# Router logits of five iterations computed with the experts stationary, four token tiles side by side on the output partitions

## What is computed

```
scores = jax.nn.softmax(xf @ Wg, axis=-1)          # Wg is 128 x 32: one column an expert
weights, indices = jax.lax.top_k(scores, TOP_K)     # TOP_K = 4 of 32 experts
...                                                 # each expert takes its first 512 token pairs
out = swiglu(xg, W1[e], W2[e], W3[e]) * w[:, None]
y = y.at[tok].add(out)
z = swiglu(xf, Ws1, Ws2, Ws3)                       # a shared expert
return (y + z)
```

## Time and profile before

| | |
|---|---|
| median of 3 runs | 824.46 us (823.9 to 824.59) |
| the profiled execution | 823.99 us, of which the span of instructions is 822.3 us |
| TensorE products (PE) | 805.6 us busy, 98% of the span |
| VectorE (DVE) | 655.5 us, 80% |
| GpSimd (POOL) | 600.2 us, 73% |
| ScalarE (ACT) | 548.9 us, 67% |
| TensorE clock granted | 1.000 of full speed over the span |

### The profile page before, as it was taken

How to read it: one execution, slowest core, us unless ns; L and a number is a source line. 1 busy time by engine, 2 the same in 40 slices (tenths; PEclk the granted TensorE clock), 3 DMA queues, 4 the chain that set the end, 5 groups by cost and what they waited for, 6 DMA issues and landing times.

```text
span 822.3 us, 12552 instructions
## 1 busy us (share of the span) xinstructions
PE 805.6 (98%) x3782; PEld 603.3 (73%) x3782; DVE 655.5 (80%) x1533; ACT 548.9 (67%) x1016; POOL 600.2 (73%) x469
## 2 busy tenths in 40 slices
PE   7899999999999999999999999999999999999997
PEld 4577877667677676777778777777777768888775
DVE  5886777898897988988787877969778899775664
ACT  3577677767567767679474985749665775777453
POOL 2168778767857677588776886877887787968775
PEclk9999999999999999999999999999999999999999
DMA  9152625425254063450544507254252534415552
GB/s 321 25 129 70 139 52 106 103 59 112 52 106 111 18 142 68 97 120 18 121 101 106 129 10 159 54 132 116 61 128 72 123 74 106 111 51 113 124 115 73
DMA packets 49331, 80.73 MB, mean 98 GB/s; under 512 B 3280, under 2 KB 14544, under 8 KB 48880
## 3 DMA queue, kind: packets, MB, share of 16 engines
q1 hardware_dynamic: 48976, 79.72, 41.8%
q10 hardware_dynamic: 288, 0.20, 0.1%
HBM read 75.19 MB, written 4.72 MB: 97 GB/s over the span
## 4 chain that ended last, share of the span: by engine, by line
PE 82%; DVE 9%; POOL 4%; issue 3%; ACT 1%; DMA 0%; POOLq 0%; DVEq 0%; ACTq 0%
PE py L869 9%; PE pb L845 7%; PE pa L845 7%; PE pb L846 7%; PE pa L846 7%; PE pb L847 7%; PE pa L847 7%; PE py L874 5%; PE py L875 4%; PE py L876 4%; PE pu L1098 3%; POOL m_h L490 3%; PE pu L970 1%; PE pv L946 1%; PE pq L1056 1%
## 5 line engine op out<-in xcount | busy, mean ns | idle before, releaser
L490 POOL TENSOR_TENSOR m_h<-m_v,m_wb 128x512 f32<-128x512 f32 x256 | 347.0, 1366 | 126.8 <-DVE m_v L1221 50.2
L580 ACT ACTIVATE m_th<-pa 128x512 f32<-128x512 f32 x240 | 141.9, 595 | 141.3 <-PE pa L847 133.7
L1221 DVE TENSOR_TENSOR m_v<-m_th,pb 128x512 f32<-128x512 f32 x224 | 151.2, 677 | 35.8 <-ACT m_th L580 16.6
L845 PE MATMUL pa<-m_xh,w1h 128*128 128x512 f32 x272 | 149.3, 549 | 0.3 <-issue 0.3
L337 POOL TENSOR_TENSOR m_hl<-m_h,m_hh 128x512 fp32r<-128x512 f32 x84 | 109.8, 1307 | 38.0 <-ACT m_hh L745 37.8
L745 ACT ACTIVATE m_hh<-m_h 128x512 fp32r<-128x512 f32 x171 | 106.9, 626 | 23.3 <-POOL m_h L490 20.4
L845 PE MATMUL pb<-m_xh,w3h 128*128 128x512 f32 x272 | 114.0, 419 | 0.9 <-DVE m_v L1221 0.7
L846 PE MATMUL pa<-m_xl,w1h 128*128 128x512 f32 x272 | 107.8, 396 | 0.0
L846 PE MATMUL pb<-m_xl,w3h 128*128 128x512 f32 x272 | 107.7, 396 | 0.0
L847 PE MATMUL pa<-m_xh,w1l 128*128 128x512 f32 x272 | 107.5, 395 | 0.0
L847 PE MATMUL pb<-m_xh,w3l 128*128 128x512 f32 x272 | 107.5, 395 | 0.0
(11 more groups left out here) (273 smaller groups left out, 1618.4 us busy)
## 6 DMA issues: line engine op xcount, KB each, us to landing
m_wb<-w_scratch SPq DMA_DIRECT2D x126, 512.0 KB, 6.7
x_sb<-in_x SPq DMA_DIRECT2D x8, 256.0 KB, 6.7
m_wb<-in_w SPq DMA_DIRECT2D x2, 1024.0 KB, 7.6
x_out<-x_sb SPq DMA_DIRECT2D x7, 256.0 KB, 6.7
u_scratch<-t_u SPq DMA_DIRECT2D x6, 256.0 KB, 2.5
t_u<-u_scratch SPq DMA_DIRECT2D x6, 256.0 KB, 2.8
f_kk<-in_w SPq DMA_DIRECT2D x1, 1024.0 KB, 10.5
w_scratch<-r_wT SPq DMA_DIRECT2D x16, 64.0 KB, 1.5
```

What stands on the lines that cost most here:

```text
L490: pool.tensor_tensor(hidden(g, p), gated(g, p), m_wb[:, p % (GRING * GP), :], ALU.mult).then_inc(sig["m_h"], 1)
L580: ins = act.activation(m_th[:, p % 2, :], pa[p % 2][:, :], ACT.Silu)
L845: pe.matmul(ps[:, :], high[:, p, :], xh, start=True, stop=False)
L1221: dve.tensor_tensor(gated(g, p), m_th[:, r, :], pb[r][:, :], ALU.mult).then_inc(sig["m_v"], 1)
```

## The change

In the five iterations with modes 4, 5 and 6 the logits products swap their operands. Before, a tile of 128 tokens was the stationary operand and the 32 columns of wg were streamed; the result lay with tokens on the partitions. Now wg is stationary (128 x 32), a tile of 128 tokens is streamed, and the four tiles go to output partitions 0 to 31, 32 to 63, 64 to 95 and 96 to 127. ScalarE copies the 128x128 result to a piece of r_wT (called r_lT in the code), and TensorE turns it back with one transpose into the next 128 columns of the same bank, where VectorE reads it. The slots of the steps behind it move.

```diff
+BY_COLUMNS = tuple(g + 1 for g in range(2 * B - 1) if MODES[g] in (4, 5, 6))
...
+        r_lT = r_wT[:, P:2 * P]
...
-                if slot == (31, 30, 32, 30, 25, 38, 23, 21)[mode]:
+                if slot == (32, 26, 29, 30, 25, 33, 21, 28)[mode]:
+                    if q in BY_COLUMNS:
+                        act.wait_ge(sig["r_lgps"], q + 1)
+                        act.activation(r_lT, router_bank(cmix)[:, 0:P], ACT.Copy).then_inc(sig["r_lT"], 1)
+                if slot == (31, 30, 32, 30, 27, 38, 23, 21)[mode]:
                     act.wait_ge(sig["r_lg"], q + 1)
...
-                        ins = pe.matmul(ps[:, E * t:E * (t + 1)], r_xT[:, P * t:P * (t + 1)], wg[:, :],
-                                        start=True, stop=True)
+                        tokens = r_xT[:, P * t:P * (t + 1)]
+                        if q in BY_COLUMNS:
+                            ins = pe.matmul(ps[E * t:E * (t + 1), 0:P], wg[:, :], tokens, start=True, stop=True)
+                        else:
+                            ins = pe.matmul(ps[:, E * t:E * (t + 1)], tokens, wg[:, :], start=True, stop=True)
                     ins.then_inc(sig["r_lgps"], 1)
+                if slot == (34, 28, 31, 32, 27, 35, 23, 28)[mode]:
+                    if q in BY_COLUMNS:
+                        pe.wait_ge(sig["r_lT"], BY_COLUMNS.index(q) + 1)
+                        pe.transpose(ps[:, P:2 * P], r_lT, ident[:, :]).then_inc(sig["r_lgt"], 1)
...
-                if slot == (30, 24, 29, 28, 22, 32, 17, 26)[mode]:
-
-                    dve.wait_ge(sig["r_lgps"], q + 1)
-                    lg = router_bank(cmix)[:, 0:T * E].rearrange("p (t e) -> p t e", t=T)
+                if slot == (30, 24, 29, 28, 27, 35, 23, 26)[mode]:
+
+                    if q in BY_COLUMNS:
+                        dve.wait_ge(sig["r_lgt"], BY_COLUMNS.index(q) + 1)
+                    else:
+                        dve.wait_ge(sig["r_lgps"], q + 1)
+                    at = P if q in BY_COLUMNS else 0
+                    lg = router_bank(cmix)[:, at:at + T * E].rearrange("p (t e) -> p t e", t=T)
...
-                if slot == (32, 29, 32, 35, 25, 38, 22, 28)[mode]:
+                if slot == (32, 29, 32, 35, 27, 38, 23, 28)[mode]:
                     dve.wait_ge(sig["r_ex"], q + 1)
...
-                if slot == (38, 34, 36, 39, 32, 38, 22, 28)[mode]:
+                if slot == (38, 34, 36, 39, 32, 38, 23, 28)[mode]:
                     constants_set()
```

More of the change, by code:

```diff
@@ L232, in hybrid_kernel @@
             "a_stats a_mvs a_vedone a_rstd a_sh a_xn a_tr a_xT a_gps a_vps a_g a_v a_s a_mx a_nm a_exp a_pT a_pTs a_o a_ri a_add "
-            "r_stats r_mvs r_vedone r_rstd r_nm r_xn r_tr r_xT m_xh m_xl r_lgps r_mx r_lg r_ex r_sum r_ri r_p r_top r_pad r_rep "
+            "r_stats r_mvs r_vedone r_rstd r_nm r_xn r_tr r_xT m_xh m_xl r_lgps r_lT r_lgt r_mx r_lg r_ex r_sum r_ri r_p r_top r_pad r_rep "
             "r_sel r_ws r_cnt r_pos r_w r_carry r_wTps r_wT w_out "
```

## The result

| | before | changed |
|---|---|---|
| median of 5 runs of each | 824.46 us (823.9 to 826.21) | 829.77 us (827.95 to 830.81) |
| the profiled execution | 823.99 us, span 822.3 | 827.95 us, span 826.1 |
| TensorE, VectorE, ScalarE, GpSimd busy | 98, 80, 67, 73% | 97, 79, 66, 72% |

The changed kernel is 0.47% slower: the ratio is 1.0047, 95% interval 1.0029 to 1.0065. The sign is as forecast; the size is not. The median is 2.7 us above the forecast of 827.1 and 0.8 above the top of its range. Execution against execution, the loss is 4.0 us where 2.7 were forecast.

The account below looks back on a forecast made before the run. TensorE's stream was taken to bound the kernel. Losses of 2.5 us (iterations 7, 9, 11), minus 0.15 (13), plus 0.38 (14) gave +2.7: 826.7 profiled, 827.1 us median (0.47 above the profiled execution before rounding), range 823.3 to 829.0.

Parts of the forecast that it names:

- d: What the new logits form takes off TensorE's four products, which ran 0.80 us as eight passes; taken as +0.26 us.
- the overlap in steps: Logits passes: a tile's second pass waits for its first, the next tile begins with that second pass; 5 x 0.107 = 0.54 us.
- The turn, 0.11: Transposing the logits back on TensorE costs 0.11 us per iteration: 0.34 to the second product after, against a 0.23 step.
- The copy costs nothing: ScalarE's copy of the logits fits in idle time or ahead of a later wait; without that cover 0.31 us.
- Iterations 7, 9 and 11, steps 1 to 7: Chain from unit 9's gate product through late exponential, a_xn, f_h and f_xl to the key product; loses 0.84 us an iteration.
- Iteration 13, the step that failed: In iteration 13 the exponential stays, its table load is already waited for, the chain to f_xl keeps order; gain 0.15 us.
- Iteration 14: VectorE has no room, so m_v(8) comes late and unit 10's linear product waits for it; loss 0.38 us.
- no overlap with a drain as well: First rival (groups don't overlap) with array drains added; put near +4.9 us when setting the range's top.
- Full overlap with the chain late: Rival: all four groups overlap fully (d = 0.59), the chain late all the same; +1.1 us, 825.6 us, chance 0.13.
- No overlap: Rival: logits groups don't overlap, or the array drains on both sides (d = -0.06); +4.4 us, 828.8 us, chance 0.15.
- The chain doesn't bind: Rival: passes overlap in steps and no wait opens; five gains of 0.15, -0.8 us, 823.7 us, chance 0.16.
- Faster: Rival: the chain doesn't bind and groups overlap fully; 5 x 0.48 = -2.4 us, 822.1 us, chance 0.10.

Follow-up runs that it names:

- experiment 5: As experiment 4, with logits, copy and turn of iterations 7, 9, 11 and 14 one place earlier and the maximum where it stood before the change: 826.17 us, ratio 1.0014.
- Experiment 8: Kernel before the change, with only ScalarE's exponential of iterations 7, 9 and 11 moved behind m_th(9): 828.22 us, ratio 1.0036.
- experiment 2: Changed kernel with the exponential of iterations 7, 9 and 11 back ahead of m_th(9), and VectorE's maximum and sum two places earlier: 830.27 us, ratio 1.0058.
- experiment 4: Changed kernel with the turn one place earlier, exponential and sum at their old places, and the maximum earlier: 825.94 us, ratio 1.0010.
- experiment 6: Changed kernel with the old logits form and old place of the maximum in iteration 13 alone: 827.49 us, ratio 1.0029.
- experiment 11: Kernel before the change, unchanged, profiled again: 824.39 us, with a TensorE wait of 1.05 us for m_v in iteration 11.
- experiment 7: Changed kernel with VectorE's sum of iterations 7, 9 and 11 moved behind m_v(9) and a_nm: 828.57 us in one run.
- the first profile: Kernel before the change, unchanged, as first profiled: execution 823.99 us.
- experiment 3: Changed kernel with all four token tiles sent to the same 32 output partitions: 830.16 us in one run.
- experiment 9: As experiment 5, with VectorE instead of ScalarE making the copy of the logits: 826.41 us, ratio 1.0019.

## Why the forecast was right in sign and short in size

- **What bounds the kernel.** Right. Nearly all of the loss is waits that opened in TensorE's stream.
- **d, and the overlap in steps.** Mis-sized: 0.26 was taken, 0.33 measured, from two errors of opposite sign. The passes took 0.35 us, not 0.54, so groups overlap more than my order of pairs allows, though less than the 0.21 of full overlap; and the entry into the narrow form costs 0.10, for which the sum had no term. That the two errors nearly cancel in d is luck. The Trainium skill (TensorEngine Tiling (Array Packing), Key Properties) says that changing the tiling mode drains TensorE. What there could be of it here is 0.10 us on entry and 0.02 on exit, less than the 0.16 each that I gave it. No run separates the entry gap from other reasons for it.
- **The turn, 0.11.** 0.12 measured.
- **"The copy costs nothing."** True in the changed kernel, where m_th(9) behind it waits 1.29 us for TensorE anyway. False in experiment 5, where the copy stands ahead of the table load.
- **Iterations 7, 9 and 11, steps 1 to 7.** Right. Gate product of unit 9 to key product: 13.25 forecast, 13.32 measured, 12.15 before. The loss was forecast at 0.84 each and measured at 0.89 in 9 and 11, 1.03 in 7. Experiment 8 shows the edit that makes it. What the steps missed is the second limit, VectorE's list, where operations are lengthened beside GpSimd. In the changed kernel it is r_sel:

```profile
423.93 1.00 DVE L1385 TENSOR_SCALAR r_sel<-r_rep 128x128 bf16<-128x128 f32 x1
```

  It cost nothing on top, but in experiment 2, where r_sel and r_ws are both lengthened, it is why the obvious repair does nothing.
- **Iteration 13, the step that failed:** "the exponential stays where it was and its table load is already waited for; the chain to f_xl keeps its order. Gain 0.15." The chain does keep its order, and f_xl was not late. But the first key product overwrites bank pv, so it also waits until VectorE has read the logits there (r_lg), and that reading had moved from ahead of a_p to behind m_v(11). VectorE's timeline in the kernel before, iteration 13:

```profile
719.36 0.29 DVE L1341 TENSOR_TENSOR r_lg<-pv,r_mx 128x128 f32<-128x128 f32 x1
719.57 1.45 DVE L1497 SCALAR_TENSOR_TENSOR a_p<-a_g,vec,a_xT 128x512 f32<-128x512 f32 x1
```

  The timelines of VectorE and then TensorE in the changed kernel, iteration 13:

```profile
722.12 1.76 DVE L1514 SCALAR_TENSOR_TENSOR a_p<-a_g,vec,a_xT 128x512 f32<-128x512 f32 x1 [0.33 <-POOL a_g L535]
...
725.07 0.68 DVE L1499 TENSOR_TENSOR f_xl<-a_p,f_xh 128x512 fp32r<-128x512 f32 x1
...
726.58 0.29 DVE L1358 TENSOR_TENSOR r_lg<-pv,r_mx 128x128 f32<-128x128 f32 x1
...
727.02 0.47 PE L1119 MATMUL pv<-f_xh,key_h 128*128 128x512 f32 x1 [1.08 <-DVE r_lg L1358]
```

  f_xl is done at 725.75; r_lg at 726.87. TensorE waits 1.08 us. Experiments 4 and 6 each move the maximum back to place 32, and the wait goes. A gain of 0.15 was forecast and a loss of 1.10 measured, so this step is worth 1.2 us. It is the largest part of the 1.8 between the 2.7 forecast and the 4.5 measured over the five iterations; 0.3 is in iterations 7, 9 and 11, 0.2 in iteration 14 and the way to it.
- **Iteration 14.** Right. 0.38 forecast, 0.46 measured from logits to counts, and a wait of 0.50 for m_v, as was said.
- **The median.** I put it 0.47 above the profiled execution, as before. It is 1.8 above. The chance meetings of experiment 11, worth 1.05 us each, are a reason for a scatter of this size. Whether the changed kernel has more of them wasn't shown. The profiled execution of the kernel before had a long tail and that of the changed kernel a short one, by 0.65 us, which makes 4.0 look nearer to 2.7 than it is.
- **The top of the range.** The time lies 0.8 us above it. The range allowed +4.9 for no overlap with a drain as well. By the prices written there (d = -0.06 - 0.33 = -0.39) that case is 3 x 1.49 + 0.50 + 1.03 = +6.0, 830.5 us.
- **The rivals.** Full overlap with the chain late (825.6) had the chain right, but d came out at 0.33 and not at 0.59. No overlap fell as well: the passes took 0.35 us and not 0.86. "The chain doesn't bind" fell. "Faster" needed d above 0.44 and no new wait, and had neither.

## What to carry to other kernels

When a read of a buffer moves to a later place, list every writer that waits for it: the next product into the same PSUM bank is one, even if it belongs to another chain. And when a repair of one limit changes nothing, look for a second one that ends at the same time; here each alone holds the product at 7.4 us from the turn (experiments 2 and 7), and the experiments that put both ScalarE's and VectorE's steps earlier (4 and 5) give part of it back, 7.0 to 7.2 against 6.74. In a kernel as tight as this a saving of 0.2 us in the stream is worth less than where the steps behind it come to lie.

## What the runs showed of the hardware

- Fp32 products with 32 stationary and 128 streamed columns: eight passes took 0.35 us in four groups of output partitions, 0.99 in one.
- Some of VectorE's operations with all operands in SBUF last until a GpSimd operation that began ahead of them is over, if that is later than their own end: r_ws and r_p take 0.29 us alone and up to 1.27 and 1.42, t_xr 0.68 alone and 1.77. A held r_ws or r_p ends 0.14 to 0.15 us after the GpSimd operation. r_sel, with one input tensor, is held too (0.23 alone, up to 1.02, ending 0.08 to 0.09 after it). Between 400 and 770 us of the 14 profiles these four meet such an operation 196 times and are held 194 times. m_v, which reads PSUM, stayed at 0.62 to 0.69 throughout. The Trainium skill (SBUF — State Buffer, Who interferes with whom) says that a VectorE instruction with two SBUF inputs contends with a GpSimd instruction that reads SBUF, and that the issue order decides who blocks. These rows agree for r_ws, r_p and t_xr, and on both sides: in the first profile it was GpSimd that waited. The two that weren't held are t_xr where GpSimd led by 0.02 and 0.03 us (experiment 3 and the first profile); r_ws was held at a lead of 0.02 (experiment 4), and from 0.04 us on every one was.
- So a few hundredths of a microsecond can cost 0.3 us (r_ws, experiment 9) or 1.05 us (t_xr, experiment 11), and TensorE's time moves in steps and not smoothly with what is ahead of it.
